# Attention stage of a two-block graph network: other places for the four additions of a step, and PSUM waits per bank

## The reference, cut to what matters

```python
edge_index = jnp.stack([src, dst])            # 50000 edges, 3125 nodes, dst sorted
mod_k = K[src] + 0.2 * rel[:, None, :]        # 4 heads of 64
scores = jnp.einsum('ehd,ehd->eh', Q[dst], mod_k) / D ** 0.5
seg_max = jax.ops.segment_max(scores, dst, num_segments=N)
ex = jnp.exp(scores - seg_max[dst])
denom = jax.ops.segment_sum(ex, dst, num_segments=N)
w = ex / denom[dst]
agg = jax.ops.segment_sum(w[:, :, None] * V[src], dst, num_segments=N)
```

## Time and profile before

| | |
|---|---|
| median of 3 runs | 4443.25 us (4440.49 to 4446.23) |
| the profiled execution's own time | 4487.6 us |
| its span | 4485.3 us |
| busy in the span: PE, DVE, ACT, POOL | 64%, 58%, 26%, 33% |
| attention stage, first gather to last addition | 1033.0 to 1877.5 us of the span |
| mean granted TensorE clock of the whole span | 0.851 of full speed |

### The profile page before, as it was taken

How to read it: one execution, slowest core, us unless ns; L and a number is a source line. 1 busy time by engine, 2 the same in 40 slices (tenths; PEclk the granted TensorE clock), 3 DMA queues, 4 the chain that set the end, 5 groups by cost and what they waited for, 6 DMA issues and landing times. The chain is left out here.

```text
span 4485.3 us, 51375 instructions
## 1 busy us (share of the span) xinstructions
PE 2850.3 (64%) x12855; PEld 1975.5 (44%) x12856; DVE 2600.5 (58%) x5649; ACT 1158.0 (26%) x4271; POOL 1490.9 (33%) x1406
## 2 busy tenths in 40 slices
PE   4555553164677777531069358888888539899970
PEld 4344443153445545221057235555555337677750
DVE  7766664245888888436721359888989820022221
ACT  0000000000555555401012024444444212233320
POOL 0377776004555555000000034444444105011114
PEclk9999999985887788565589679999999759999995
DMA  0000002515665666010000033333333126211112
GB/s 29 2 4 4 4 4 9 74 57 166 177 183 172 176 176 175 29 66 2 14 20 0 25 110 108 104 103 105 106 102 107 42 70 102 47 33 34 33 36 75
DMA packets 236031, 323.43 MB, mean 72 GB/s; under 512 B 114940, under 2 KB 166560, under 8 KB 235609
## 3 DMA queue, kind: packets, MB, share of 16 engines
q0 software_dynamic: 83488, 220.74, 18.9%
q1 hardware_dynamic: 117971, 95.44, 8.0%
q10 hardware_dynamic: 34402, 5.30, 1.0%
HBM read 287.87 MB, written 32.86 MB: 72 GB/s over the span
## 5 line engine op out<-in xcount | busy, mean ns | idle before, releaser
L1253 POOL DMA_INDIRECT g_rows<-h_d,src x416 | 397.1, 954 | 1328.0 <-SPq L1200 812.8
L925 POOL DMA_INDIRECT a_strip<-kv_d,src x416 | 430.4, 1035 | 593.8 <-POOLq L74 262.4
L484 POOL DMA_INDIRECT rec_d<-rec_s,place x400 | 476.2, 1191 | 243.6 <-issue 216.8
L949 ACT ACTIVATE x<-a_strip,x 128x64 f32<-128x64 f32 x1664 | 408.5, 334 | 221.6 <-PE a_psv L994 197.6
L994 PE MATMUL a_psv<-x 128*125 128x260 f32 x832 | 306.2, 502 | 158.0 <-DVE agg L1088 121.0
L384 PE MATMUL ps_base<-start,lo_hot_t 125*125 125x25 f32 x800 | 184.7, 384 | 264.1 <-DVE picked L439 263.4
L384 PEld LDWEIGHTS ps_base<-start,lo_hot_t 125*125 125x125 f32 x800 | 175.4, 326 | 341.2 <-issue 339.7
L1330 PE MATMUL g_psa<-g_msg,g_hot 128*125 128x256 f32 x832 | 249.7, 426 | 109.3 <-DVE g_msg L1422 109.3
L1318 PE MATMUL g_pso<-w_o,g_ut 128*128 128x256 f32 x832 | 284.3, 424 | 1.9 <-ACT g_lk L1268 1.9
L1590 PE MATMUL ps_h_f<-h_t,w_f 128*128 x640 | 174.5, 434 | 161.7 <-DMA b_f<-in_L_ffn_b 136.8
L994 PEld LDWEIGHTS a_psv<-x 128*125 128x125 f32 x832 | 178.2, 238 | 221.9 <-DVE agg L1088 118.1
(11 more groups left out here) (373 smaller groups left out, 5661.7 us busy)
## 6 DMA issues: line engine op xcount, KB each, us to landing
a_row<-rows_d SPq DMA_DIRECT2D x104, 256.0 KB
e_w<-in_L_ffn_W1p SPq DMA_DIRECT2D x8, 1024.0 KB
e_w<-in_L_ffn_W2p SPq DMA_DIRECT2D x8, 1024.0 KB
y_d<-e_y SPq DMA_DIRECT2D x56, 128.0 KB, 1.7
a_strip<-kv_d,src POOLq DMA_INDIRECT x416
g_rows<-h_d,src POOLq DMA_INDIRECT x416
rec_d<-rec_s,place POOLq DMA_INDIRECT x400
x<-in_x SPq DMA_DIRECT2D x2, 3125.0 KB
```

The costliest lines, as they stand in the source:

```text
L484: pool.indirect_dma_start(out=m.rec_d[:, :], out_offset=bass.IndirectOffsetOnAxis(ap=place[b][:, u:u + 1], axis=0), in_=rec_s[b][:, u, :], ...
L925: pool.indirect_dma_start(out=strip[:, lane.start + u, place:place + 2, :].rearrange("p a d -> p (a d)"), out_offset=None, in_=m.kv_d[:, : ...
L949: act.activation(msg[b][:, u, h, 0:HD], strip[:, lane.start + u, place, h * HD:(h + 1) * HD], ACT.Copy, scale=w[:, k * U + u, h:h + 1])
L1253: pool.indirect_dma_start(out=rows[r][:, u, 64:512], out_offset=None, in_=m.h_d[:, :], in_offset=bass.IndirectOffsetOnAxis(ap=m.src[:, s * ...
```

## The change

`added` no longer counts the rescales; they signal a semaphore of their own, `s_scaled`, which only VectorE's first addition of a group waits for. PE waits before each aggregate matmul, for the addition that empties that matmul's bank (`added(s, u) - 1`, the addition two before). VectorE's loop is put in another order and runs one turn longer (`STEPS + LAG + 2`): the additions of edge tiles 2 and 3 are made in the next step, around `modify`; `one_hot` comes before `multiply`, and so do the register load and the rescale; the additions of tiles 0 and 1 come after `multiply` and after `total`.

```diff
         def added(s, u):
-            return 1 + s * U + u + s // CS
+            return 1 + s * U + u
@@ aggregate, on PE
                     pe.wait_ge(s_hot, s + 1)
                     pe.wait_ge(s_wv, s + 1)
-                pe.wait_ge(s_add, added(s, 2 * half))
                 for u in (2 * half, 2 * half + 1):
+                    pe.wait_ge(s_add, added(s, u) - 1)
                     pe.matmul(ps_v[u % 2][:, 0:H * HW], hot[b][:, u, :],
@@ add, on VectorE
-            def add(s, us, tiles):
-                for u in us:
-                    dve.wait_ge(s_mm, s * U + u + 1)
-                    dve.wait_ge(s_add, added(s, u))
-                    agg = m.agg[:, tiles[u], :, :].rearrange("p h d -> p (h d)")
-                    dve.tensor_tensor(agg, agg, ps_v[u % 2][:, 0:H * HW], ALU.add).then_inc(s_add, 1)
+            def add(s, u, tiles):
+                if s < 0:
+                    return
+                dve.wait_ge(s_mm, s * U + u + 1)
+                dve.wait_ge(s_add, added(s, u))
+                if u == 0 and s >= CS and s % CS == 0:
+                    dve.wait_ge(s_scaled, s // CS)
+                agg = m.agg[:, tiles[u], :, :].rearrange("p h d -> p (h d)")
+                dve.tensor_tensor(agg, agg, ps_v[u % 2][:, 0:H * HW], ALU.add).then_inc(s_add, 1)
@@ rescale, on VectorE
-                dve.wait_ge(s_add, added(c * CS, 0) - 1)
+                dve.wait_ge(s_add, added(c * CS, 0))
                 dve.tensor_tensor(m.agg[:, j, :, :], m.agg[:, j, :, :], fac[:, :, None].to_broadcast([P, H, HW]),
-                                  ALU.mult).then_inc(s_add, 1)
+                                  ALU.mult).then_inc(s_scaled, 1)
@@ VectorE's loop
-            for now in range(STEPS + LAG + 1):
+            tiles = None
+            for now in range(STEPS + LAG + 2):
...
                 if k == 1 and linked:
                     raise_top(c)
+                add(v - 1, 2, tiles)
                 if now < STEPS:
                     modify(now)
+                add(v - 1, 3, tiles)
+                if 0 <= now - LAG < STEPS:
+                    one_hot(now - LAG)
+                if 0 <= v < STEPS:
+                    tiles = node_tiles(v, ENGINE.DVE)
+                    if v and v % CS == 0:
+                        rescale(v // CS)
+                if now < STEPS:
                     multiply(now)
-                if v >= 0 and v % CS == 0 and v:
-                    rescale(v // CS)
-                if v >= 0:
-                    tiles = node_tiles(v, ENGINE.DVE)
-                    add(v, (0, 1), tiles)
                 if k == 0 and linked:
                     across(c)
+                if v < STEPS:
+                    add(v, 0, tiles)
                 if now < STEPS:
                     total(now)
...
-                if 0 <= now - LAG < STEPS:
-                    one_hot(now - LAG)
-                if v >= 0:
-                    add(v, (2, 3), tiles)
+                if v < STEPS:
+                    add(v, 1, tiles)
```

More of the change, by code:

```diff
@@ L893, in build_attention @@
         s_add = sem("a_add")
+        s_scaled = sem("a_scaled")
         s_link = sem("a_link")
```

## The result

| | before | after |
|---|---|---|
| median, us | 4444.74 (4 runs, 4440.49 to 4450.39) | 4343.93 (4 runs, 4341.52 to 4346.03) |
| ratio | 1 | 0.9772, 95% interval 0.9755 to 0.9789 |
| the profiled execution | 4487.6 | 4341.52 |

A forecast was written before the change was run, and what follows sets the result against it. VectorE, busy 88% of the steady part, was taken to set the pace. Terms of 71.6 + 18 - 11 - 6.4 + 11.5 = 84 us, taken from 4443.25, gave 4359 us, range 4334 to 4400.

The forecast's parts named there:

- Additions apart, and `multiply` away from `modify`: VectorE's ordinary step: 0.58 us from separating two pairs of additions, 0.19 from moving `multiply`; 93 x 0.77 = 71.6 us gained.
- The register load: Load moved ahead of `multiply` on VectorE: taken as hidden, no cost; the rival that it is bare, 4391 us, chance 0.05.
- The rescale: VectorE's waits for PE behind a rescale go: 1.5 us for each of 12 rescales, 18 us gained.
- The new wait of the copy: At a group's first step VectorE's copy of the turned scores waits for PE: 0.85 us in 13 groups, 11 us lost.
- PE between the additions: New waits of VectorE on PE, 1.65 us a group, against 1.1 that go: net 6.4 us lost over 11.6 groups.
- the opposite: PE, fed more evenly, stays at full clock, no new waits in ordinary steps: 108 us gained, 4335 us; chance 0.14.
- The drain: With a wait per bank, drain steps fall from 5.50 to 4.35 us; with two at 0.6, 11.5 us gained.
- GpSimd and the transfers: Gathers need 5.4 us a step against 5.74: no cost; the rival that they hold 6.5, 4425 us, chance 0.04.
- The rival at half clock: TensorE falls to half clock and becomes the bound, PE needing about 7.75 us a step: slower, 4516 us; chance 0.04.

The follow-up runs named there:

- r5: The changed kernel, but the addition of tile 1 stands right behind that of tile 0, ahead of the reduce; 4363.28 us, ratio 0.9816.
- r6: The changed kernel, but `multiply` stands right behind `modify`; 4377.21 us, ratio 0.9851.
- r3: The changed kernel, but PE waits for both additions ahead of each half of the aggregation, as before; 4433.42 us, ratio 0.9974.
- r2: The kernel before, in its old order, with waits per bank on PE and the rescale not waited for by PE; 4416.49 us, ratio 0.9938.
- r8: The changed kernel with the register load back behind `multiply`; 4346.20 us, ratio 0.9778.
- r4: The kernel before, but the rescale signals its own semaphore and PE does not wait for it; 4438.62 us, ratio 0.9978.
- r7: The changed kernel, but PE waits again for the rescale ahead of a group's first aggregate matmul; 4353.42 us, ratio 0.9791.
- r1: The kernel before, unchanged, run again for a second profile; 4446.09 us.

## Why the prediction was right

The direction, the mechanism and the range were right, and the forecast was 15 us short (4359 against 4344). By its own steps:

- *Additions apart, and `multiply` away from `modify`.* Forecast 0.77 us a step, measured 0.79 (6.51 to 5.72). The parts taken singly: 0.32 for one pair (r5, forecast 0.29) and 0.19 for `multiply` (r6, forecast 0.19). This term, 71.6 us, carried the sum and stands. But it holds only together with the wait per bank, which the text did not say: the same order with the old waits leaves a step of 6.31 (r3), and the wait per bank in the old order one of 6.51 (r2). Singly they give 12 and 29 us, together 101.
- *The register load.* Forecast nothing, measured nothing (r8).
- *The rescale.* Forecast 1.5 us each. The step fell by 2.23 in the median, 0.79 of it from the order, so 1.44 is left. Taking away the wait gave 1.03 of it by itself (r4), and with the rescale's new place the wait could nearly as well have stayed (r7).
- *The new wait of the copy.* Forecast 0.85, measured 0.51. Turning and signal went faster than summed up: the copy started 0.31 after PE's turning did.
- *PE between the additions.* Within a forecast that came true, this step failed. It took 1.65 us a group of new waits against 1.1 that go; measured are 0.24 a group of waits for PE in place of 2.5. The prediction took half clock for about as frequent as before, but the granted clock rose from 0.81 to 0.92, the case called the opposite, at 0.14. In place of 6.4 us lost there is about nothing, and no gain either: of the 2.3 us a group that went, 1.44 stand under the rescale and some 0.8 were waits of second additions, which the term for additions apart has already.
- *The drain.* Forecast 11.5 us, measured 18.4. ScalarE's step was taken at 3.93 + 0.21 and signals, 4.35; its small activation overlaps with the next and the step is 3.92. And TensorE ran at full clock for about two thirds of it (0.84 in the mean).
- *GpSimd and the transfers.* No cost, and none was measured: the DMA share rose to 0.70, and no wait of VectorE on a gather is in the steady part.

With the measured sizes in the prediction's own sum it is 0.79 x 93 + 1.44 x 12 - 0.51 x 13 + 18.4 = 73.5 + 17.3 - 6.6 + 18.4 = 102.6 us, and the stage got 102.3 shorter. (One of the twelve rescales lies in the drain and the last copy waits longer than the others, so the two agree to some 2 us, not better.) That the forecast of 84 was low comes from PE's waits (6 us), the drain (7) and the copy (4), and for the rest from 0.79 in place of 0.77.

One sum of the prediction is wrong: by its own 4.3 and 7.75 us a step, PE's mean need passes 6.51 when the clock is at half for (6.51 - 4.28) / (7.75 - 4.28) = 0.64 of the time, not for four fifths. That rival was nearer than the text says, though at 0.40 and then 0.16 of the time the clock stayed well clear of it.

The rival at half clock, the one that would have made it slower, did not come. The rule of the Trainium skill named beside it (TensorE: Matmul & The Clock Gate, "A second HAM failure mode: psum-queue depth-cycling") has idle times between matmul groups that go round the PSUM banks make the clock swing. It does swing here, in every kernel, but four short waits instead of two longer ones went with a higher clock, both in the new order (0.84 in r3, 0.92 in the changed kernel) and in the old one (0.81 to 0.86, and 0.50 to 0.83 in the drain).

That the higher clock followed from the shorter idle times of PE, and was not brought about by something else in the step, was not tested by itself. What is shown is that it does not set the ordinary step: 6.51 us at 0.81 and at 0.86 (r1, r2), 6.31 at 0.84 (r3).

## What to carry to other kernels

Read start to start on the engine that sets the pace: an instruction that needs the result right ahead of it costs two or three tenths of a microsecond that no idle row of its own may show, and other work put in between takes them back. A new order on one engine needs the other engine's waits to be as fine as the order is: count for each wait which single buffer it must have empty, since a wait for a pair can undo the gain. Where two engines hand buffers to each other, try the two halves of such a change singly and together; their sum says little about both.

## What was not expected of the hardware

The drain's stretch ran at a granted clock of 0.50 from end to end in the three kernels with waits per half (before, r3, r4; PE busy for 47 of 64 to 65 us) and at 0.81 to 0.84 in the mean in all those with a wait per bank ahead of tile 2 (PE busy for 33 to 34 of 42 to 48 us, with the same matmuls). What makes the difference is open: PE's busy time is itself longer at half clock. Two profiles of the same kernel differed by 37 us in one stage, most of it four waits for a transferred row at the start of the stage; in a second profile they were not there, and a first profile alone would have put them into the difference.
